# A fused decoder layer: self-attention with centred weights, scores on row halves, another order on VectorE and TensorE

## The chip, the cores and the metric

The kernel is one program on one core of a Trainium2 chip. The metric is the device time of one execution in microseconds (us). Engines are named as in the profile: PE is TensorE's matmuls (PEld its weight loads), DVE is VectorE, ACT is ScalarE, POOL is GpSimd, SP is SyncE.

## The reference, cut to what matters

One decoder layer on x of shape 4 x 512 x 256: causal self-attention with a squared feature map (16 heads of 16 features), cross-attention to 1601 context rows, and a top-2 mixture of 8 experts, with a layer norm after each. Only the first part is touched:

```python
def _feature_map(x, gamma, beta):                 # x: one head's 16 features
    mu = x.mean(axis=-1, keepdims=True)
    var = ((x - mu) ** 2).mean(axis=-1, keepdims=True)
    xn = (x - mu) / jnp.sqrt(var + LN_EPS) * gamma + beta
    ...
q = hidden @ Wq.T ; k = hidden @ Wk.T ; v = hidden @ Wv.T      # 16 heads x 16
phi_q, phi_k = _feature_map(q), _feature_map(k)
# causal: num = phi_q . cumsum(phi_k v), den = phi_q . cumsum(phi_k) + EPS
y = num / den ; return y @ Wo.T
```

The features' inner product is the square of (xn_q . xn_k) / 4, so the kernel squares a score matrix instead of forming 136 features.

## The kernel before, in words

**Stages.** Self-attention of all four batches comes first (0 to about 331 us of the profile), then cross-attention, then the experts. Every engine runs its own hand-written list of instructions in order, and semaphores join them.

**Slots.** A batch of 512 tokens has four row tiles of 128 and four quads of four heads. A batch runs as 16 slots, slot n = 4g + c: quad g, key tile c. In slot n PE makes the scores of slot n+1 (L1417, four heads, 512, 384, 256 or 128 query columns for c = 0 to 3) into PSUM banks 4 and 5 in turn, ACT squares them into A (L751), POOL masks the diagonal block (L550), and PE multiplies the values of slot n into bank 6 (L1427). DVE copies bank 6 out at a quad's end (`quad_out`, L1010).

**Work alongside.** `alongside` (L422) hangs other steps on the slots, and each engine walks the same list. *rest*: the last steps of the batch before (back, yt, out, stats, rsqrt, norm) in slots 0 to 7. *own*: transposes of later quads' q and k (`turn`, L1398; ACT copies qT, DVE copies kT). *ahead*: the features of the next batch. For each row tile i PE projects q and k (`project_qk`, bank 2, six 512-column matmuls) and v (`project_v`, bank 3, six 256-column ones) in slot 2i+1. In slot 2i+2 DVE centres (`centre`: sum, scale, subtract, L954 to L958) and ACT copies v and squares the centred values (L692, L694). In slot 2i+3 DVE forms the variance, in slot 2i+4 ACT takes the root (`deviation`, L698) and DVE normalises (L973 to L980), in slot 2i+5 DVE applies gamma and beta, and slots 9 to 12 split the result into high and low parts. Batches 0 to 2 carry such work for the next one; batch 3 carries weight casts instead.

**Waits that matter.** `project_qk` of tile i waits for `cen_ok` of tile i-1, since bank 2 must be read. A score matmul waits for the square that last read its bank, two matmuls earlier. The opening (L448) runs the same steps for batch 0 before any slot, tile by tile. kT holds four slabs a quad: each head's keys on its own 64 rows with zeros on the other 64 (two memsets, L935 and L936), so a score matmul contracts over 128 rows and DVE copies each transposed pair twice (L1003, L1004).

## Time and profile before

| what | value |
|---|---|
| median of the timed runs | 1490.67 us (1488.88 to 1492.04, 3 runs) |
| the profiled execution | 1501.86 us, its span 1500.1 us, mean granted clock 0.899 |
| PE busy / DVE / ACT / POOL | 83% / 50% / 39% / 46% of the span |
| self-attention, first to last instruction | about 335 us |
| one batch of self-attention, with the next one's features alongside | about 65 to 72 us |

Read the page for the shares first, then the stretches of self-attention alone, then the timeline of one batch. PE's busy time is modelled from pipelined matmuls, so the starts of instructions are the safer numbers. A timeline row is: start, duration, engine, line, operation, tiles, shape, count, and in brackets the idle time before it with what ended it.

### The profile page before, as it was taken

The numbers are of one execution on the slowest core, as the hardware profiler recorded it, in microseconds if no ns is written. First come the engines' busy times: TensorE is split into PE (matmuls) and PEld (weight loads), VectorE is DVE, ScalarE is ACT, GpSimd is POOL, SyncE is SP. The second block draws the span as 40 slices with busy tenths as digits, with TensorE's granted clock in tenths as the row PEclk, the third lists the DMA queues.
The fourth block names the chain that finished last, engine by engine and source line by source line (L and its number), as shares of the span: only waits on it lengthen the run. The fifth ranks groups of instructions, "written<-read, shape, count | busy, mean of one in ns | idle before, by whom it ended". The sixth has DMA issues, their size and how long they took to land.

```text
span 1500.1 us, 20297 instructions
## 1 busy us (share of the span) xinstructions
PE 1243.3 (83%) x6416; PEld 712.3 (47%) x6416; DVE 754.2 (50%) x1328; ACT 582.5 (39%) x999; POOL 684.5 (46%) x597
## 2 busy tenths in 40 slices
PE   3488778856999899998999989999994449999970
PEld 3355454534554445544455444554543426666640
DVE  6475858536335753458624665446423432222217
ACT  3364555632444544445434444444441012222210
POOL 0132323420467674676655766666794431111111
PEclk8688897966999999999999999999996569999995
DMA  5580000010000100000000000000002921111113
GB/s 172 197 270 16 1 0 0 1 45 11 1 0 1 36 10 1 1 1 23 22 2 1 1 11 23 1 0 1 1 1 83 316 68 42 44 46 42 45 43 143
DMA packets 33007, 64.66 MB, mean 43 GB/s; under 512 B 4221, under 2 KB 22398, under 8 KB 32640
## 3 DMA queue, kind: packets, MB, share of 16 engines
q1 hardware_dynamic: 23200, 32.41, 6.6%
q10 hardware_dynamic: 6304, 22.59, 4.7%
q0 software_dynamic: 3408, 8.43, 1.6%
q8 instruction: 55, 0.90, 0.2%
q14 instruction: 40, 0.33, 0.1%
HBM read 52.89 MB, written 28.34 MB: 54 GB/s over the span
## 4 chain that ended last, share of the span: by engine, by line
PE 60%; DVE 20%; issue 10%; ACT 3%; POOL 2%; DMA 2%; another core or an unknown queue 1%; ACTq 1%; SPq 0%; DVEq 0%; POOLq 0%
PE PS L1582 11%; PE PS L1689 9%; PE PS L1510 9%; PE PS L1593 8%; DVE mxp L1168 5%; PE PS L1706 5%; PE PS L225 3%; PE PS L1417 2%; PE PS L1523 2%; PE PS L226 2%; PE PS L227 2%; DVE R L1148 2%; PE PS L1406 2%; PE PS L1427 2%; POOL acc L608 1%
## 5 line engine op out<-in xcount | busy, mean ns | idle before, releaser
L608 POOL TENSOR_TENSOR acc<-acc,PX 128x1024 f32<-128x1024 f32 (+1 forms) x176 | 421.2, 2393 | 161.1 <-ACT PX L846 155.2
L846 ACT ACTIVATE PX<-PS 128x1024 f32<-128x1024 f32 (+1 forms) x208 | 212.9, 1025 | 247.2 <-PE PS L1582 236.4
L1168 DVE TENSOR_REDUCE mxp<-PS 128x2 f32<-128x804 f32 x256 | 240.4, 986 | 132.3 <-PE PS L1523 131.9
L1593 PE MATMUL PS<-PX,V 128*64 128x512 f32 (+1 forms) x832 | 226.3, 623 | 0.0
L550 POOL TENSOR_SCALAR_AFFINE_SELECT A<-A 128x128 f32<-128x128 f32 x256 | 88.8, 359 | 219.8 <-ACT A L751 216.2
L1689 PE MATMUL PS<-W,XBT 128*128 x312 | 149.6, 603 | 1.3 <-ACT XBT L902 1.3
L751 ACT ACTIVATE A<-PS 128x512 f32<-128x512 f32 (+3 forms) x256 | 99.3, 437 | 98.0 <-PE PS L1417 90.9
L669 POOL DMA_INDIRECT Y<-yb,goal_u x39 | 38.4, 986 | 201.8 <-DVE yb L1327 196.7
L1417 PE MATMUL PS<-qT,kT 128*128 128x512 f32 (+3 forms) x256 | 88.0, 420 | 27.0 <-ACT A L751 21.9
L1582 PEld LDWEIGHTS PS<-QH,KH 64*128 64x128 f32 (+1 forms) x416 | 38.4, 181 | 151.3 <-issue 89.9
L1582 PE MATMUL PS<-QH,KH 64*128 64x512 f32 (+1 forms) x416 | 104.6, 499 | 3.5 <-issue 2.2
L1523 PE MATMUL PS<-KH,QH 64*128 64x402 f32 x512 | 79.0, 369 | 18.5 <-DVE mxp L1168 18.5
L1582 PE MATMUL PS<-QH,KL 64*128 64x512 f32 (+1 forms) x416 | 83.3, 395 | 0.0
L1582 PE MATMUL PS<-MR,one_row 64*128 64x512 f32 (+1 forms) x416 | 83.2, 393 | 0.0
L1582 PE MATMUL PS<-QL,KH 64*128 64x512 f32 (+1 forms) x416 | 83.2, 395 | 0.0
L1417 PEld LDWEIGHTS PS<-qT,kT 128*128 128x128 f32 x256 | 48.9, 218 | 64.3 <-ACT A L751 47.6
L605 POOL TENSOR_TENSOR acc<-PX 128x1024 f32<-128x1024 f32 x16 | 38.0, 2376 | 90.5 <-ACT PX L846 90.5
L1689 PEld LDWEIGHTS PS<-W,XBT 128*128 128x128 f32 x312 | 57.2, 194 | 43.3 <-issue 41.4
L1706 PE MATMUL PS<-W,hT 128*128 x312 | 73.9, 380 | 0.8 <-ACT hT L915 0.8
L1321 DVE TENSOR_TENSOR hm<-PS,gl 128x512 f32<-128x512 f32 x39 | 27.0, 691 | 94.2 <-PE PS L1689 94.2
L1193 DVE TENSOR_TENSOR X<-PS,X 128x512 f32<-128x512 f32 (+1 forms) x32 | 22.1, 692 | 102.9 <-PE PS L227 102.8
L829 ACT COPY V<-PS 128x512 f32<-128x512 f32 (+1 forms) x52 | 30.5, 587 | 103.7 <-PE PS L1510 103.7
(261 smaller groups left out, 2138.9 us busy)
## 6 DMA issues: line engine op xcount, KB each, us to landing
W<-in_w SPq DMA_DIRECT2D x24, 512.0 KB
XB<-XG ACTq DMA_DIRECT2D x39, 129.0 KB, 2.1
yl<-Y SPq DMA_DIRECT2D x4, 1024.0 KB, 9.0
X<-in_x SPq DMA_DIRECT2D x1, 2048.0 KB, 12.1
out<-X SPq DMA_DIRECT2D x4, 512.0 KB, 2.9
xt_raw<-in_xt SPq DMA_DIRECT2D x3, 512.0 KB, 4.4
c_raw<-in_ctxt SPq DMA_DIRECT2D x6, 200.0 KB, 2.4
c_raw<-in_ctxt SPq DMA_DIRECT2D x12, 100.0 KB, 2.6
```

The costliest lines, as they stand in the source:

```text
L550: pool.affine_select(out=blk, in_=blk, compare_op=ALU.is_ge, fill=0.0, base=0, pattern=[[1, P]], channel_multiplier=-1).then_inc(mask_ok, 1)
L608: ins = pool.tensor_tensor(sums[0:r], sums[0:r], PX[0:r, (NL * p + t) % NP, :, :], ALU.add)
L751: act.activation(A[:, u % 8, P * c:T], PS[:, 4 + u % 2, P * c:T], ACT.Square, scale=0.25).then_inc(sqr_ok, 1)
L846: act.activation(PX[0:r, u % NP, :, :], PS[0:r, score_buffer(u):score_buffer(u) + 2, :], ACT.Exp, scale=XD ** -0.5)\
L1168: dve.tensor_reduce(mxp[:, p % 2, :, v % NT, v // NT:v // NT + 1].rearrange("p a o -> p (a o)"), PS[:, k:k + 2, 0:BW], AX, ALU.max)\
L1417: pe.matmul(PS[:, 4 + u % 2, P * c:T], kT[:, g % 2, j, P * c:P * c + P], qT[:, g % 2, j // 2, P * c:T], start=True, stop=True).then_inc(sc ...
L1510: mm = pe.matmul(o, l, r, start=(n == 0), stop=(n == len(ops) - 1))
L1523: mm = pe.matmul(bank(bk + half, BW), QH[rows, p % 2, P * i:P * i + P], KH[rows, p % 2, BSTART[k]:BSTART[k] + BW], start=True, stop=True)
L1582: mm = pe.matmul(bank(score_buffer(u) + half, rows=r), lhs, q_[rows, p % 2, :], start=(n == 0), stop=(n == 3))
L1593: mm = pe.matmul(PS[rows, 4, :], V[0:LROWS[j], j, P * p + XD * half:P * p + XD * half + XD], PX[0:LROWS[j], u % NP, half, :], start=(j == ...
L1689: mm = pe.matmul(bank(2 * m + j % 2), XBT[:, j % 2, c, :], W13[:, bass.ds(e, 1), m, c, :].rearrange("p o n -> p (o n)"), start=(c == 0), s ...
L1706: mm = pe.matmul(bank(6, D), hT[:, j % 2, f, :], W2[:, bass.ds(e, 1), f, :].rearrange("p o n -> p (o n)"), start=(f == 0), stop=(f == FC - 1))
```

## The change

1. **Centred weights.** Subtracting a head's mean over its 16 features is linear, so DVE centres the columns of Wq and Wk once, ahead of the casts (two sums, a scale, two additions of 128x512). `centre` goes on DVE. ACT squares bank 2 directly. `normalise` now multiplies the projection in PSUM, so it is the last reader of the bank: `project_qk` of tile i waits for `nrm_ok` of tile i-1.
2. **Row halves.** kT has two slabs without zeros (the memsets go). The two heads of a pair are two matmuls on 64 rows each, into banks 4 and 5; ACT squares both banks in one instruction; a pair of scores waits for the squares of the pair before. DVE copies kT once.
3. **Order.** In `alongside` the variance moves to slot 2i+2, normalise to 2i+3, gamma and beta to 2i+4. On DVE a slot's feature steps come ahead of `quad_out`. On PE projections come last in a slot, behind the value products. The opening goes two tiles at a time, with bank 6 as a second bank.

```diff
-            for i in range(NT):
-                for after, kind in ((1, "project v"), (1, "project qk"), (2, "centre"), (3, "variance"), (4, "normalise"), (5, "affine")):
+            for i in reversed(range(NT)):
+                for after, kind in ((1, "project v"), (1, "project qk"), (2, "variance"), (2, "centre"), (3, "normalise"), (4, "affine")):
...
+        for two in ((0, 1), (2, 3)):
+            OPENING += [(kind, i) for i in two for kind in FEATURES[0:3]] + [("variance", i) for i in two]
+            OPENING += [("split", i - 2) for i in two if i >= 2]
+            OPENING += [("normalise", i) for i in two] + [("affine", i) for i in two]
...
# ACT
-                act.wait_ge(cen_ok, NT * t + i + 1)
-                act.activation(feat[:, i, :], cen[:, i % 2, :], ACT.Square).then_inc(sq_ok, 1)
+                act.wait_ge(qk_mm, NT * t + i + 1)
+                act.activation(feat[:, i, :], bank(qk_bank(t, i)), ACT.Square).then_inc(sq_ok, 1)
...
-                for j in range(4):
-                    u, c = 4 * n + j, n % NT
-                    act.wait_ge(sc_mm, 64 * b + u + 1)
+                for two in range(2):
+                    u, c = 4 * n + 2 * two, n % NT
+                    act.wait_ge(sc_mm, 64 * b + u + 2)
...
-                    act.activation(A[:, u % 8, P * c:T], PS[:, 4 + u % 2, P * c:T], ACT.Square,
-                                   scale=0.25).then_inc(sqr_ok, 1)
+                    act.activation(A[:, u % 8:u % 8 + 2, P * c:T], PS[:, 4:6, P * c:T], ACT.Square,
+                                   scale=0.25).then_inc(sqr_ok, 2)
...
# DVE
-            dve.memset(as32(kT[64:P, :, 0:4:2, :]), 0.0).then_inc(const_dve, 1)
-            dve.memset(as32(kT[0:64, :, 1:4:2, :]), 0.0).then_inc(const_dve, 1)
+            dve.wait_ge(ld_q, 16)
+            for c in range(KC):
+                ins = dve.tensor_reduce(w_mean[:, c, :], groups[c], AX, ALU.add)
+            ins.then_inc(wch, 1)
+            dve.wait_ge(wch, 1)
+            dve.tensor_scalar(w_mean[:, :, :], w_mean[:, :, :], -1.0 / SF, None, ALU.mult).then_inc(wch, 1)
+            dve.wait_ge(wch, 2)
+            for c in range(KC):
+                ins = dve.tensor_tensor(groups[c], groups[c], w_mean[:, c, :].unsqueeze(2).broadcast_to([P, 32, SF]), ALU.add)
...
-                dve.tensor_tensor(v, v, rs.unsqueeze(2).broadcast_to([P, 32, SF]), ALU.mult).then_inc(nrm_ok, 1)
+                if started(t, i, 2):
+                    dve.wait_ge(feat_ok, NT * t + i - 1)
+                dve.tensor_tensor(v, bank(qk_bank(t, i)).rearrange("p (g f) -> p g f", f=SF), rs.unsqueeze(2).broadcast_to([P, 32, SF]), ALU.mult).then_inc(nrm_ok, 1)
...
-                dve.tensor_copy(kT[0:64, g % 2, 2 * q, :], bank(1, rows=64)).then_inc(kT_ok, 1)
-                dve.tensor_copy(kT[64:P, g % 2, 2 * q + 1, :], PS[64:P, 1, :]).then_inc(kT_ok, 1)
+                dve.tensor_copy(kT[:, g % 2, q, :], bank(1)).then_inc(kT_ok, 1)
...
-                    if n % NT == NT - 1:
-                        quad_out(b, n // NT)
                     for d, s in steps:
                         if s[0] not in LATE and s[0] != "x":
                             step(b + d, s)
+                    if n % NT == NT - 1:
+                        quad_out(b, n // NT)
...
# PE
-                if started(t, i, 1):
-                    pe.wait_ge(cen_ok, NT * t + i)
+                if isinstance(t, int) and t == 0:
+                    if i >= 2:
+                        pe.wait_ge(nrm_ok, i - 1)
+                else:
+                    pe.wait_ge(nrm_ok, NT * t + i)
...
                 if started(b, u, 2):
-                    pe.wait_ge(sqr_ok, 64 * b + u - 1)
-                pe.matmul(PS[:, 4 + u % 2, P * c:T], kT[:, g % 2, j, P * c:P * c + P],
-                          qT[:, g % 2, j // 2, P * c:T], start=True, stop=True).then_inc(sc_mm, 1)
+                    pe.wait_ge(sqr_ok, 64 * b + u)
+                for half in range(2):
+                    rows = slice(64 * half, 64 * half + 64)
+                    pe.matmul(PS[:, 4 + half, P * c:T], kT[rows, g % 2, two, P * c:P * c + P],
+                              qT[rows, g % 2, two, P * c:T], start=True, stop=True).then_inc(sc_mm, 1)
...
-                    half = (len(steps) + 1) // 2
+                    steps.sort(key=lambda ds: ds[1][0] in ("project qk", "project v"))
+                    half = min((len(steps) + 1) // 2, sum(s[0] not in ("project qk", "project v") for d, s in steps))
```

PE, batch 0, slots 2 and 3, before: the scores of slot 4 (128x512), the two transposes (q and k of a head pair), slot 3's values (32x128) and the projection of tile 1 of the next batch. xt_h and xt_l are the high and low parts of x, WSh and WSl those of the weights, QX and KX the features, VS the values, A the squared scores.

```order
L1417 MATMUL PS<-qT,kT 128x512 [waits sqr_ok,kT_ok,qT_ok]
L1417 MATMUL PS<-qT,kT 128x512 [waits sqr_ok]
L1406 MATMUL PS<-ident,QX 128x128 [waits qT_ok]
L1406 MATMUL PS<-ident,QX 128x128 x3
L1406 MATMUL PS<-ident,KX 128x128 [waits kT_ok]
L1406 MATMUL PS<-ident,KX 128x128 x3
L1417 MATMUL PS<-qT,kT 128x512 [waits sqr_ok] x2
L1427 MATMUL PS<-A,VS 32x128 [waits mask_ok] x4
L225 MATMUL PS<-WSh,xt_h 128x512 [waits cen_ok,xt_lo]
L226 MATMUL PS<-WSl,xt_h 128x512
```

The same place now:

```order
L1426 MATMUL PS<-qT,kT 128x512 [waits sqr_ok,kT_ok,qT_ok]
L1426 MATMUL PS<-qT,kT 128x512
L1412 MATMUL PS<-ident,QX 128x128 [waits qT_ok]
L1412 MATMUL PS<-ident,QX 128x128 x3
L1412 MATMUL PS<-ident,KX 128x128 [waits kT_ok]
L1412 MATMUL PS<-ident,KX 128x128 x3
L1426 MATMUL PS<-qT,kT 128x512 [waits sqr_ok]
L1426 MATMUL PS<-qT,kT 128x512
L1436 MATMUL PS<-A,VS 32x128 [waits mask_ok] x4
L225 MATMUL PS<-WSh,xt_h 128x512 [waits nrm_ok,xt_lo]
L226 MATMUL PS<-WSl,xt_h 128x512
```

The projection stood behind `cen_ok` of tile 0, from slot 2; it now stands behind `nrm_ok` of tile 0, which DVE gives in slot 3 itself. Both scores of a pair now share one wait.

DVE, batch 0, slots 2 and 3, before: centring of tile 0 (L954 to L958), the quad's values out (L1010), variance, the two kT copies.

```order
L954 TENSOR_REDUCE g_mean<-PS 128x32 [waits qk_mm]
L955 TENSOR_SCALAR g_mean<-g_mean 128x32 [waits cch]
L958 TENSOR_TENSOR cen<-PS,g_mean 128x512 [waits feat_ok,cch]
L1010 COPY osb<-PS 128x512 [waits av_mm]
L963 TENSOR_REDUCE g_var<-feat 128x32 [waits sq_ok]
L965 TENSOR_SCALAR g_var<-g_var 128x32 [waits vch]
L1003 CAST kT<-PS 64x512 [waits tk_mm]
L1004 CAST kT<-PS 64x512
```

The same place now:

```order
L967 TENSOR_REDUCE g_var<-feat 128x32 [waits sq_ok]
L969 TENSOR_SCALAR g_var<-g_var 128x32 [waits vch]
L977 RECIPROCAL g_rs<-g_sd 128x32 [waits sd_ok]
L978 TENSOR_TENSOR g_t<-g_rs 128x32 [waits fch]
L979 TENSOR_TENSOR g_t<-g_t,g_var 128x32 [waits fch]
L980 TENSOR_SCALAR g_t<-g_t 128x32 [waits fch]
L981 TENSOR_TENSOR g_rs<-g_rs,g_t 128x32 [waits fch]
L986 TENSOR_TENSOR cen<-PS,g_rs 128x512 [waits feat_ok,fn_ok]
L1015 COPY osb<-PS 128x512 [waits av_mm]
L1009 CAST kT<-PS 128x512 [waits tk_mm]
```

The whole of normalise (`g_rs` to `cen<-PS,g_rs`) moved one slot forward, ahead of the quad's copy, and centring is gone.

## Rows read from the trace of the kernel before

**Rows 1.** Busy time by stretch: two quads of batch 2, one of batch 3
```profile
core 0: us, PE busy (x) PEld busy (x) DVE busy (x) ACT busy (x) POOL busy (x), PEclk, DMA share, GB/s
197.90:216.60 18.70, 15.36 (x105) 10.60 (x105) 8.24 (x15) 9.73 (x25) 5.40 (x16) 0.91 0.00 0
236.50:255.40 18.90, 15.10 (x76) 8.09 (x75) 17.31 (x41) 12.14 (x31) 6.92 (x19) 0.74 0.00 0
269.50:281.80 12.30, 11.29 (x90) 7.55 (x91) 5.67 (x11) 7.96 (x22) 4.30 (x15) 1.00 0.00 1
```

**Rows 2.** Waits of batch 2: engine line waited for, us, times, longest
```profile
ACT A L751 <- PE PS L1417: 27.3, 23, 5.2
...
ACT feat L694 <- DVE cen L958: 3.6, 2, 2.6
...
PE PS L225 <- DVE xt_l L942: 2.2, 1, 2.2
```

**Rows 3.** Timeline, PE (start, us): first value products of slots 0, 8, 0; 0, 3, 8, 0
```profile
63.49 1.08 PE L1427 MATMUL PS<-A,VS 128*32 128x512 f32 x4
...
99.89 1.06 PE L1427 MATMUL PS<-A,VS 128*32 128x512 f32 x8
...
128.75 0.64 PE L1427 MATMUL PS<-A,VS 128*32 128x512 f32 x4
...
200.05 1.06 PE L1427 MATMUL PS<-A,VS 128*32 128x512 f32 x8
...
216.01 0.42 PE L1427 MATMUL PS<-A,VS 128*32 128x128 f32 x8
...
240.19 1.07 PE L1427 MATMUL PS<-A,VS 128*32 128x512 f32 x8
...
271.62 1.07 PE L1427 MATMUL PS<-A,VS 128*32 128x512 f32 x8
```

**Rows 4.** Timeline, all engines, around the second projection of batch 2
```profile
215.36 0.72 PE L1417 MATMUL PS<-qT,kT 128*128 128x512 f32 x2
...
215.88 1.09 ACT L751 ACTIVATE A<-PS 128x512 f32<-128x512 f32 x2 [2.63 <-PE PS L1417]
...
216.36 0.50 PE L225 MATMUL PS<-WSh,xt_h 128*128 128x512 f32 x1
```

**Rows 5.** The page's costliest groups: ScalarE reading two banks at once
```profile
L846 ACT ACTIVATE PX<-PS 128x1024 f32<-128x1024 f32 (+1 forms) x208 | 212.9, 1025 | 247.2 <-PE PS L1582 236.4
```

**Rows 6.** Timeline, ACT and DVE: deviation to the end of normalise
```profile
244.17 0.21 ACT L698 ACTIVATE g_sd<-g_var 128x32 f32<-128x32 f32 x1
...
244.41 0.35 DVE L973 RECIPROCAL g_rs<-g_sd 128x32 f32<-128x32 f32 x1 [0.81 <-ACT g_sd L698]
...
245.69 0.69 DVE L980 TENSOR_TENSOR cen<-cen,g_rs 128x512 f32<-128x512 f32 x1
```

**Rows 7.** Timeline, PE: two projection matmuls of the third projection of batch 2
```profile
226.98 0.63 PE L226 MATMUL PS<-WSl,xt_h 128*128 128x512 f32 x1
...
227.41 0.63 PE L227 MATMUL PS<-WSh,xt_l 128*128 128x512 f32 x1
```

**Rows 8.** Timeline, PE, cross-attention: matmul pairs on row halves
```profile
509.78 0.50 PE L1582 MATMUL PS<-QH,KH 64*128 64x512 f32 x2
...
510.12 0.40 PE L1582 MATMUL PS<-QL,KH 64*128 64x512 f32 x2
...
510.35 0.40 PE L1582 MATMUL PS<-QH,KL 64*128 64x512 f32 x2
```

**Rows 9.** Timeline, the opening: ACT's first cast, PE's first matmul, first transposes
```profile
6.45 1.47 ACT L680 CAST WSh<-raw 128x1536 fp32r<-128x1536 f32 x1 [3.82 <-DMA raw<-in_wqkv]
...
11.00 0.77 PE L225 MATMUL PS<-WSh,xt_h 128*128 128x512 f32 x1 [11.00 <-DVE xt_l L942]
...
48.09 1.12 PE L1406 MATMUL PS<-ident,QX 128*128 128x128 f32 x4 [15.67 <-DVE KX L998]
```

**Rows 10.** Timeline, PE: a transpose behind the second copy of kT
```profile
241.99 0.55 PE L1406 MATMUL PS<-ident,KX 128*128 128x128 f32 x3 [0.73 <-DVE kT L1004]
```

More of the change, by code:

```diff
@@ L765, in _ @@
                 if s == ("x",):
+                    act.wait_ge(wch, 3)
+                    act.copy(WSh[:, :, 0:3 * D], raw[:, 0:2, 0:3 * D]).then_inc(w_hi, 1)
                     act.wait_ge(ld_w, 16 * N_LDW)
@@ L1408, in turn, with scores @@
                 mm.then_inc(done, 1)
-            def score(b, n, j):
-                g, c, u = n // NT, n % NT, 4 * n + j
-                if c == 0 and j == 0:
+            def scores(b, n, two):
+                g, c, u = n // NT, n % NT, 4 * n + 2 * two
+                if c == 0 and two == 0:
                     pe.wait_ge(qT_ok, 8 * b + 2 * g + 2)
-                    pe.wait_ge(kT_ok, 16 * b + 4 * g + 4)
+                    pe.wait_ge(kT_ok, 8 * b + 2 * g + 2)
                 if started(b, u, 2):
-                    pe.wait_ge(sqr_ok, 64 * b + u - 1)
-                pe.matmul(PS[:, 4 + u % 2, P * c:T], kT[:, g % 2, j, P * c:P * c + P],
-                          qT[:, g % 2, j // 2, P * c:T], start=True, stop=True).then_inc(sc_mm, 1)
+                    pe.wait_ge(sqr_ok, 64 * b + u)
[3 more added lines that the diff above has]
+                              qT[rows, g % 2, two, P * c:T], start=True, stop=True).then_inc(sc_mm, 1)
             def value(b, n, j):
@@ L1476, in attention @@
                     steps = [(d, s) for d, s in alongside(n, first, more) if s[0] in PE_STEPS]
-                    half = (len(steps) + 1) // 2
-                    for j in range(4):
+                    steps.sort(key=lambda ds: ds[1][0] in ("project qk", "project v"))
+                    half = min((len(steps) + 1) // 2, sum(s[0] not in ("project qk", "project v") for d, s in steps))
+                    for two in range(2):
                         if n + 1 < SLOTS:
-                            score(b, n + 1, j)
+                            scores(b, n + 1, two)
                         elif more:
-                            score(b + 1, 0, j)
-                        if j == 1:
+                            scores(b + 1, 0, two)
+                        if two == 0:
                             for d, s in steps[:half]:
@@ L1492, in _ @@
                 step(0, s)
-            for j in range(4):
-                score(0, 0, j)
+            for two in range(2):
+                scores(0, 0, two)
             attention(0, True, True)
```

49 lines of the change are left out of this document (19 added, 30 removed).

## The prediction

> **What bounds the kernel now.** The change touches self-attention alone, so the page's shares of the whole span say little. I read the busy times of single quads first [rows 1], then the waits of batch 2 [rows 2], then the timeline of that batch [rows 3, 4]. In [rows 1] no engine is full: PE is the busiest (15.4 of 18.7 us), but its busy time is modelled and overlaps. The one other full engine is DVE in a quad with feature work, 17.3 of 18.9 us. [rows 2] says ACT waits 27.3 us of a batch for score matmuls. So a batch is a chain of hand-overs: PE scores, ACT squares, PE again, and PE's in-order steps stand between. What counts is what a step puts on PE's queue between two score pairs. [rows 3] gives the lengths of it: batch 2 takes 200.05 to 271.62, 71.6 us, of which slots 0 to 3 take 16.0, slots 3 to 8 24.2 and slots 8 to the next 0 31.4. Batch 0 takes 65.3 (63.49 to 128.75). The profiled execution is 11.2 us above the median; I sum changes against it and move them to the median unscaled.
>
> **The new wait, worked out.** PE's projection of tile i (slots 3, 5, 7) now waits for normalise of tile i-1 in the same slot. DVE needs ACT's root for that, and the root stands on ACT behind the squares of this slot's last score pair. So from that pair's start the chain is: 0.52 us until ACT starts (215.36 to 215.88) [rows 4], 1.03 for a square over two banks of 512 [rows 5], 2.21 from the root to the end of normalise (244.17 to 245.69 + 0.69) [rows 6]: 3.76 us. Before, the projection started 1.00 us after that pair (216.36) [rows 4]. That is +2.76 in slots 3 and 7. In slot 5 the pair is 256 wide: about 0.41 + 0.55 + 2.21 = 3.17, less some 1.0 of value products and pair that PE has anyway, +2.2. Together **+7.7 us a batch**. Queued behind the wait are the v projection and then the next slot's scores, so ACT, POOL and DVE run dry as well: nothing covers it. Ends: +4 if a third of each chain falls where PE waited anyway, +9 if in slot 5 DVE is still at the layer statistics.
>
> **The clock of those projections.** A 512-column matmul steps by 0.43 us at the lower level (1.2 GHz) [rows 7], which here stands behind a PE wait, and by 0.23 at the higher (2.4 GHz) [rows 8]. A tile's q, k and v are six of 512 and six of 256 columns: 2.1 us or 3.8. After a wait of 2 to 3 us I expect the lower level for part of each: take +1.0 for each of three, **+3.0**, ends 0 and +5.1.
>
> **What is taken away.** (a) In slot 1 PE sat 2.2 us before the first projection for xt_l [rows 2], ahead of the second score pair; now pair and values come first and fill it: **-1.5**, ends 0 and -2.2. (b) ACT's square waited 3.6 us a batch for centring [rows 2], once 2.6 us in slot 8 with the score squares behind it; now it reads PSUM: **-2.5**, ends 0 and -3.6. Centring itself (some 1.6 us a tile on DVE) is otherwise hidden, and so costs nothing to remove. (c) The second kT copy is 0.7 us. Where a transpose waits for it (0.73) [rows 10], at slots 8 and 15 and the quad's turn, it goes: **-2.1**, ends 0 and -5.5 (all eight).
>
> **Score pairs.** In cross-attention two matmuls on row halves step together by 0.23 us for 512 columns (510.12 to 510.35) [rows 8], so a pair takes what one took. Where PE sets the pace (quads 0 and 1, 10240 columns) half goes: 2.3 at full clock, take **-2.0**. Against it: before, PE refilled one bank while ACT squared the other, and ACT could run two squares in 1.09 us without a gap [rows 4]. Now both banks are freed at once, and a pair costs 1.03 + 0.52 + 0.15 (hand-over, my estimate) = 1.70: +0.61 at 512 wide, less when other ACT work fills the gap. Take +0.4 for 8 of a batch's 32 pairs, **+3.2**, ends 0 and +6. DVE's order (feature steps before the quad's copy) adds a delay of osb, which the value products of the next quad reach later than the projection; hidden, up to 0.7 a quad if not.
>
> **Sum of a batch with features alongside:** 7.7 + 3.0 - 1.5 - 2.5 - 2.1 - 2.0 + 3.2 = **+5.8**. Laying the slots of batch 2 out by hand with these durations gives 14.4, 33.0 and 29.5 us against 16.0, 24.2 and 31.4: +5.3, where the last stretch is 27.2 at the higher clock throughout and about 31 at the lower. Three such batches: +17.4.
>
> **Batch 3** has no projections. 20 exposed pairs x 0.4 = 8.0, half the columns of four quads -4.6, one kT copy a quad -2.9: **+0.5**, ends -5 and +6. In [rows 1] its quad has the full clock and PE 11.3 of 12.3 us busy, so PE-paced pairs are many there.
>
> **The opening.** Centring the weights is two sums, a scale and two additions, about 3.0 us on DVE by the 0.69 us of a 128x512 operation [rows 6], ahead of ACT's first cast at 6.45 [rows 9]; it hides nothing, so PE starts at 13.9 instead of 11.0. The memsets that go ended before the weights landed: nothing. DVE then leaves out four centrings (6.2 us), but going by pairs of tiles it waits about 2.6 us for the second square of each pair. The transposes, at 48.09 [rows 9] behind DVE's last split, come about 0.6 earlier, and one kT copy helps once: **-1.0**, ends -4 and +3.
>
> **Total:** 17.4 + 0.5 - 1.0 = +16.9, that is 1518.8 for an execution like the profiled one and **1507.6 for the median**.
>
> **A rule beside the rows.** The first pair on row halves after matmuls of another tile shape took 0.34 us to the next, the following 0.23 [rows 8]: 0.11 for the change of shape. Score pairs now differ in shape from the transposes and output matmuls between them, some 24 more changes a batch. The Trainium skill, "TensorEngine Tiling (Array Packing)", section "Key Properties", says that changing the tiling mode, not merely the tile, drains the engine; that speaks against this change, and by it the row's 0.11 would be paid at each. I left it out of the sum since most such changes fall where PE waits for ACT; it is a rival below.
>
> **Rivals.**
> - *The gains meet a high clock (no change).* No lower level at the projections (0 for 3.0) and half the exposed pairs: 1.2 a batch, 3.6 - 1.0 - 3.5 (batch 3) = -0.9: 1489.8. For it: quad 0 of batch 2 had 0.91 of the full clock [rows 1]. Against: the new waits are longer than the ones before. 0.12.
> - *DVE's queue is the pace (faster).* In quads 1 and 2 DVE is 17.3 of 18.9 us busy [rows 1]. If its backlog sets their length, three centrings (4.7) and four copies (2.8) come off, and two of the three new waits lie within DVE's own queue and cost nothing: -7.5 + 2.8 = -4.7 a batch, -14.1 - 1.0 = -15: 1475.6. It decides if DVE's idle there, 1.6 us, is all the slack there is. Against: only 3.6 us of ACT's waiting names centring [rows 2]; the rest names PE. 0.16.
> - *The lower clock stays.* PE works less, waits longer and is at 1.2 GHz through most of a batch: projections +5.1, exposed pairs +6.0, some +0.4 more: 11 a batch, +33, batch 3 +4.5, opening -1: 1527. [rows 1] has 0.74 in one quad already. 0.08.
> - *Every change of shape is paid* at 0.11: 2.6 a batch, 9.7 in all: 1517. 0.04.
>
> **How the numbers follow.** The forecast has 0.60 (slower), and its own range by the ends above is about 1497 to 1518. Faster has 0.16 from DVE's queue and 0.02 from the forecast's low ends; within 0.2% (3 us, about what a measurement of this kernel can tell from no change) 0.12 and 0.01; slower 0.69. The range goes from 1480, which leaves out most of the DVE case, to 1522, which leaves out the lasting low clock: together about 0.17.
>
> **What would show it.** In the trace after: PE idle of 2 to 3 us before the first q/k projection matmul in slots 3, 5 and 7, named as a wait for normalise; slots 3 to 8 of batch 2 at 31 to 34 us, slots 0 to 3 at 14.5; no ACT wait for DVE in slot 8; PE's first matmul near 13.9 and the first transposes near 47.5. It is wrong if those waits are under 1 us, which would mean that ACT reaches the root sooner than the last pair allows, or if slots 8 to 0 fall below 26 us.

## The result, and the profile after

The changed kernel takes 1522.02 us, median of four runs (1520.49 to 1523.09), against 1489.78 us for the kernel before (1486.94 to 1492.04, four runs). The ratio is 1.0217, 95% interval 1.0196 to 1.0237: 32 us slower. The profiled execution took 1520.49 us. The forecast had the direction, but +17 us (1507.6) instead of +32; 1522.02 lies just outside its range of 1480 to 1522.

Read self-attention by batch first. These are the busy times of the kernel after, each stretch (from:to, its length, then the engines' busy us and counts) from a batch's first value products to the next one's. The last one ends at the last copy of a quad (L1015).

```profile
core 0: us, PE busy (x) PEld busy (x) DVE busy (x) ACT busy (x) POOL busy (x), PEclk, DMA share, GB/s
60.35:131.19 70.84, 52.37 (x322) 29.88 (x321) 33.06 (x73) 35.60 (x65) 19.98 (x65) 0.84 0.57 189
131.19:210.28 79.09, 58.85 (x355) 35.64 (x353) 38.60 (x91) 36.69 (x67) 20.72 (x66) 0.81 0.03 8
210.28:288.38 78.10, 57.30 (x354) 34.88 (x352) 38.51 (x91) 36.49 (x67) 20.89 (x66) 0.83 0.00 0
288.38:338.79 50.41, 39.89 (x266) 19.00 (x264) 18.61 (x39) 26.69 (x41) 18.44 (x61) 0.80 0.12 34
```

The same view of a second execution of the kernel before (1495.36 us, profiled beside the experiments):

```profile
62.09:125.74 63.65, 51.61 (x322) 31.46 (x321) 44.02 (x91) 37.86 (x98) 21.14 (x64) 0.88 0.65 218
125.74:197.80 72.06, 57.48 (x353) 35.97 (x353) 50.96 (x113) 39.45 (x100) 24.65 (x65) 0.86 0.03 9
197.80:268.85 71.05, 57.31 (x353) 35.84 (x353) 50.23 (x109) 39.17 (x100) 23.95 (x65) 0.86 0.00 0
268.85:311.16 42.31, 36.93 (x265) 21.11 (x264) 22.73 (x46) 28.42 (x70) 20.43 (x59) 1.00 0.09 26
```

I use this second execution as the base from here on. The one that the prediction had read took 1501.86 us and 65.3, 71.3, 71.6 and 44.7 us for the four batches ([rows 3]; the last one ends with the copy at 316.4). The second took 63.7, 72.1, 71.1 and 42.3. After is 70.8, 79.1, 78.1 and 50.4: +7.2, +7.0, +7.1 and +8.1, or 29.4, less 1.7 in the opening (the first column starts at 60.35 instead of 62.09). DVE's busy time fell by 11 to 12 us in each of the first three batches and PE has nearly the same number of matmuls as before (the counts in brackets), yet every batch is longer. The first three have a granted clock (PEclk) of 0.84, 0.81 and 0.83 instead of 0.88, 0.86 and 0.86. Batch 3 has 0.80 instead of 1.00.

Where in a batch? Starts of value products of the kernel after, batch 2, slots 0, 3, 8 and the next 0, which answer to [rows 3]:

```profile
210.28 1.25 PE L1436 MATMUL PS<-A,VS 128*32 128x512 f32 x8
...
224.06 0.43 PE L1436 MATMUL PS<-A,VS 128*32 128x128 f32 x8
...
260.90 1.07 PE L1436 MATMUL PS<-A,VS 128*32 128x512 f32 x8
...
288.38 1.06 PE L1436 MATMUL PS<-A,VS 128*32 128x512 f32 x8
```

Slots 0 to 3 take 13.8, slots 3 to 8 36.8, the rest 27.5. In the second execution of before they took 15.9, 24.3 and 30.8 (batches 0 and 1 go the same way: slots 3 to 8 take 32.3 and 35.3 instead of 21.5 and 24.2). The first and last stretch gained 2.2 and 3.3; the middle, where the projections of tiles 1 to 3 stand, lost 12.5. Here is its first projection, slot 3 of the kernel after; it answers to [rows 4, 6]:

```profile
223.63 0.49 PE L1426 MATMUL PS<-qT,kT 64*128 64x512 f32 x2
...
224.25 1.02 ACT L755 ACTIVATE A<-PS 128x1024 f32<-128x1024 f32 x1 [3.29 <-issue]
...
225.17 0.22 ACT L702 ACTIVATE g_sd<-g_var 128x32 f32<-128x32 f32 x1
...
225.42 0.35 DVE L977 RECIPROCAL g_rs<-g_sd 128x32 f32<-128x32 f32 x1 [4.33 <-ACT g_sd L702]
...
226.79 0.69 DVE L986 TENSOR_TENSOR cen<-PS,g_rs 128x512 f32<-128x512 f32 x1
...
227.53 0.80 PE L225 MATMUL PS<-WSh,xt_h 128*128 128x512 f32 x1 [3.05 <-DVE cen L986]
...
228.13 0.63 PE L226 MATMUL PS<-WSl,xt_h 128*128 128x512 f32 x1
...
231.67 0.69 PE L1426 MATMUL PS<-qT,kT 64*128 64x384 f32 x2
...
232.56 0.81 ACT L755 ACTIVATE A<-PS 128x768 f32<-128x768 f32 x1 [6.70 <-PE PS L1426]
```

The score pair starts at 223.63 and ACT squares both banks (224.25). Only then comes the root (225.17), DVE works from 225.42 to the end of `cen`, and PE, done with the value products at about 224.5, starts the projection at 227.53 after 3.05 us of nothing. The matmuls that follow take 0.63 us each and step by 0.43 (228.13, then 228.56), the 1.2 GHz level. The projection is through after 4.14 us. The next score pair stands behind all twelve, at 231.67, and ACT waited 6.70 us for it. From score pair to score pair that is 8.04 us. In the kernel before the same stretch took 3.21:

```profile
213.10 0.72 PE L1417 MATMUL PS<-qT,kT 128*128 128x512 f32 x2
...
216.31 0.52 PE L1417 MATMUL PS<-qT,kT 128*128 128x384 f32 x2
```

The waits between 60 and 310 us say that this is not one place. Kernel after:

```profile
ACT A L755 <- PE PS L1426: 99.9, 66, 7.3
...
PE PS L225 <- DVE cen L986: 25.7, 9, 3.1
```

Kernel before:

```profile
ACT A L751 <- PE PS L1417: 84.6, 83, 5.2
...
ACT feat L694 <- DVE cen L958: 11.5, 6, 2.6
...
PE PS L225 <- DVE xt_l L942: 6.9, 3, 2.6
```

Nine waits for `cen` (three a batch) hold 25.7 us of PE. ACT's 11.5 us for centring and PE's 6.9 us for `xt_l` are gone. ACT's wait for scores grew by 15.3. The twelve matmuls of the nine projections in slots 3, 5 and 7 took 35.0 us together, from the first of them to what PE starts next, against 22.4 for the same matmuls in the second execution of before.

### The profile page after: what moved, and what is told of

The parts are those of the page before. It is cut to its first block, busy times and chain, and to the rows that moved or that the text cites. A ratio compares the mean times of both kernels' runs of the same rounds, so it can differ in the third digit from the quotient of the medians.

```text
span 1518.7 us, 19910 instructions
## 1 busy us (share of the span) xinstructions
PE 1242.6 (82%) x6416; PEld 701.8 (46%) x6416; DVE 708.2 (47%) x1251; ACT 572.1 (38%) x871; POOL 672.8 (44%) x597
## 4 chain that ended last, share of the span: by engine, by line
PE 51%; DVE 12%; issue 7%; POOL 4%; DMA 2%; ACT 2%; SPq 0%; DVEq 0%; ACTq 0%; POOLq 0%
PE PS L1592 11%; PE PS L1699 9%; PE PS L1520 9%; PE PS L1603 8%; DVE mxp L1171 5%; PE PS L1716 4%; PE PS L1533 2%; POOL XG L669 2%; DVE R L1151 2%; PE PS L225 2%; POOL acc L614 1%; PE PS L1708 1%; DVE Cc L1121 1%; PE PS L1573 1%; DMA c_raw<-in_ctxt 1%
## 5 line engine op out<-in xcount | busy, mean ns | idle before, releaser
L556 POOL TENSOR_SCALAR_AFFINE_SELECT A<-A 128x128 f32<-128x128 f32 x256 | 78.6, 328 | 254.2 <-ACT A L755 253.8
L755 ACT ACTIVATE A<-PS 128x1024 f32<-128x1024 f32 (+3 forms) x128 | 90.4, 706 | 149.2 <-PE PS L1426 113.6
L1426 PE MATMUL PS<-qT,kT 64*128 64x512 f32 (+3 forms) x256 | 59.9, 464 | 39.7 <-ACT A L755 35.8
L1533 PEld LDWEIGHTS PS<-KH,QH 64*128 64x128 f32 x512 | 50.1, 191 | 42.9 <-DVE mxp L1171 31.9
```

The costliest lines, as they stand in the source:

```text
L556: pool.affine_select(out=blk, in_=blk, compare_op=ALU.is_ge, fill=0.0, base=0, pattern=[[1, P]], channel_multiplier=-1).then_inc(mask_ok, 1)
L755: act.activation(A[:, u % 8:u % 8 + 2, P * c:T], PS[:, 4:6, P * c:T], ACT.Square, scale=0.25).then_inc(sqr_ok, 2)
L1426: pe.matmul(PS[:, 4 + half, P * c:T], kT[rows, g % 2, two, P * c:P * c + P], qT[rows, g % 2, two, P * c:T], start=True, stop=True).then_in ...
L1533: mm = pe.matmul(bank(bk + half, BW), QH[rows, p % 2, P * i:P * i + P], KH[rows, p % 2, BSTART[k]:BSTART[k] + BW], start=True, stop=True)
```

## The experiments

Four questions: is it the wait, how much of it is the clock, what is the rest of the change worth, and can the gain be had. Each timed kernel is compared with runs of the kernel before on its own chip, whose medians were 1498.04, 1495.66 or 1497.82 us (1489.78 for the result above). So ratios are given, and a difference in us is that of two ratios times 1496. They are the recorded estimates with their 95% intervals; two medians divided can come out up to 0.002 away (0.9868 and not 0.9884 for the last row of the table), so nothing is read from differences that small. The table also has the end of self-attention and the length of its batches in each trace. What follows the last copy of a quad is the same in all and took 1177 to 1188 us, so a few us between two ratios prove little unless the traced batches agree.

| kernel | ratio | self-attention ends | batches 0 to 2 | batch 3 |
|---|---|---|---|---|
| before (second execution) | 1 | 311.2 | 206.8 | 42.3 |
| after | 1.0217, 1.0202 | 338.8 | 228.0 | 50.4 |
| after, bank copied early | 0.9998 | 311.8 | 199.3 | 51.2 |
| after, PE kept busy | 1.0137 | 322.2 | 211.6 | 49.4 |
| after, root first | 1.0112 | 329.5 | 216.6 | 51.4 |
| after, a square a bank | 1.0111 | 333.4 | 229.1 | 44.2 |
| after, old DVE order | 1.0174 | 343.5 | 233.8 | 49.6 |
| root first, a square a bank, old DVE order | 1.0141 | 330.1 | 225.4 | 44.7 |
| before, row halves alone | 1.0024 | 312.8 | 202.3 | 47.4 |
| before, centred weights alone | 0.9961 | 307.7 | 201.5 | 43.6 |
| early copy, a square a bank | 0.9932 | 301.7 | 197.1 | 44.4 |
| the same, old DVE order | 0.9884 | 294.3 | 190.9 | 43.6 |

**The control.** The kernel after, unchanged, beside the second group.

> The changed kernel once more, unedited, on the chip of the runs beside it, as their yardstick. The runs of a1 to a4 shared a chip on which the kernel before took 1498 us, not 1490. If the change costs the same there: ratio 1.02 to the kernel before, and its self-attention ends at 339 us of the profile as in the first one, give or take 4.

Ratio 1.0202 (1.0176 to 1.0227), +30 us; its trace has self-attention ending within 0.2 us of the first one (338.62), while all behind that took 1186.5 us instead of 1179.9. The kernel before, once more, for its trace:

> The kernel before once more, unedited, for a second profile. In the first one its self-attention ended (last copy of a quad) at 316.4 us, with 71.3 and 71.6 us for batches 1 and 2. If the granted clock falls by chance, these move by a few us (311 to 321), and the low clock sits at other slots.

1495.36 us. Its self-attention is 5.2 us shorter than in the first execution, and 2.4 of them lie in the last quad of batch 3. Busy times of that quad in the second execution:

```profile
303.09:311.16 8.07, 6.90 (x48) 3.32 (x48) 2.77 (x5) 5.01 (x14) 4.34 (x14) 1.00 0.48 133
```

And in the first:

```profile
305.87:316.35 10.48, 9.30 (x48) 4.38 (x48) 2.77 (x6) 5.00 (x14) 4.39 (x14) 0.67 0.53 152
```

It took 8.1 us at a granted clock of 1.00, against 10.5 at 0.67.

**The wait alone removed.** DVE copies the bank before normalise, so the bank is free early; centred weights, row halves and both orders stay.

> The changed kernel with one thing put back: DVE copies the projection of a tile out of PSUM in slot 2i+2 (one 128x512 copy, some 0.7 us), and the next projection waits for that copy and for the square, not for normalise in its own slot. Theory A (PE's wait for normalise in slots 3, 5 and 7, and the low clock of the projections behind it, is the loss): slots 3 to 8 of batch 2 fall from 36.8 us to about 22 to 25, three batches give back 33 to 40 us, so 1483 to 1490. Rival B (what costs is that both score banks are freed together): the wait goes but the time stays above 1515. Rival C (the loss is spread over the new order of steps): half of it comes back, about 1505.

```diff
+            def centre(t, i):                                  # DVE, slot 2i+2, ahead of variance
+                dve.wait_ge(sq_ok, NT * t + i + 1)
...
+                dve.tensor_copy(cen[:, i % 2, :], bank(qk_bank(t, i))).then_inc(cen_ok, 1)
...
-                dve.tensor_tensor(v, bank(qk_bank(t, i)).rearrange("p (g f) -> p g f", f=SF), rs...
+                dve.tensor_tensor(v, v, rs...
...
-                    pe.wait_ge(nrm_ok, NT * t + i)             # PE, project_qk
+                    pe.wait_ge(cen_ok, NT * t + i)
+                    pe.wait_ge(sq_ok, NT * t + i)
```

Ratio 0.9998 (0.9982 to 1.0014): the whole loss is gone, with one more 0.69 us copy a tile on DVE. The same slot in its trace (score pair, projection, next score pair):

```profile
206.40 0.79 PE L1435 MATMUL PS<-qT,kT 64*128 64x512 f32 x2
...
207.48 0.50 PE L225 MATMUL PS<-WSh,xt_h 128*128 128x512 f32 x1
...
209.78 0.44 PE L1435 MATMUL PS<-qT,kT 64*128 64x384 f32 x2
```

3.38 us from pair to pair. No PE wait for DVE's `cen` is left, and the projection is through in 2.30 us (207.48 to 209.78) instead of 4.14. (One of its nine projections, in slot 5 of batch 1, still ran at the lower level and took 3.99 us.) So the wait with what follows it costs 30 to 33 us by the ratios (1.0202 or 1.0217 less 0.9998) and 28.7 by the traces of batches 0 to 2 (228.0 less 199.3), 3.2 to 3.6 for each of nine. Not all of what the rows show is net: slots 3 to 8 of the three batches lost 35.2 us of their length with the copy (104.5 to 69.3), while their other slots grew by 6.4 (123.5 to 130.0). The cost of the added copies is in these numbers too and was not measured by itself.

**The wait kept, PE kept busy.** Fourteen matmuls of 256 columns, whose result nobody reads, fill the wait.

> The changed kernel, with 14 matmuls of 256 columns into an unused half of bank 3 put before PE's wait for normalise in slots 3, 5 and 7 (their result is not read). They fill 1.6 us of the wait at 2.4 GHz, 3.0 at 1.2 GHz. If the clock of the projections is a price of its own (a projection took 4.1 us there against 2.1), nine projections come back by up to 2 us: about 1504 to 1510. If the granted clock does not rise, or the wait alone is the loss: 1520 or, with the filler late, up to 1530.

```diff
+                    for _ in range(14 if i >= 1 else 0):
+                        pe.matmul(PS[:, 3, D:2 * D], xt_h[:, 0, 0:P], WSh[:, 0, 0:D], start=True, stop=True)
                     pe.wait_ge(nrm_ok, NT * t + i)
```

Ratio 1.0137 (1.0120 to 1.0154). The same slot in its timeline: score pair, filler, first projection matmul, next score pair.

```profile
214.66 0.50 PE L1428 MATMUL PS<-qT,kT 64*128 64x512 f32 x2
...
215.45 1.93 PE L1388 MATMUL PS<-WSh,xt_h 128*128 128x256 f32 x14
...
218.57 0.50 PE L225 MATMUL PS<-WSh,xt_h 128*128 128x512 f32 x1 [1.20 <-DVE cen L986]
...
220.89 0.44 PE L1428 MATMUL PS<-qT,kT 64*128 64x384 f32 x2
```

The projection starts 3.91 us after the pair, as without filler (3.90), so DVE's `cen` comes no sooner. But it is through after 2.32 us (218.57 to 220.89) instead of 4.14, and pair to pair is 6.23 us instead of 8.04. Busy times from slot 3 to slot 8 of batch 2, this kernel:

```profile
215.09:245.48 30.39, 24.42 (x177) 17.53 (x175) 19.06 (x51) 10.70 (x20) 6.24 (x21) 1.00 0.00 0
```

The kernel after:

```profile
224.06:260.90 36.84, 25.80 (x135) 17.69 (x133) 19.05 (x51) 10.69 (x20) 6.35 (x21) 0.72 0.00 0
```

Clock 1.00 against 0.72, and 30.4 us against 36.8, with work added. All nine projections are at the higher level now (20.6 us together instead of 35.0). The low clock therefore costs 10 to 12 us by the ratios and 16.4 by the traces of batches 0 to 2: a third of what the wait costs by the one, over half by the other. The rest is idle time.

**Root first.** If ACT takes the root ahead of the slot's squares, normalise need not wait for them.

> The changed kernel with one ACT step moved: the root (`deviation`) of slot 2i+3 ahead of that slot's squares, not behind them. Nothing is copied, and PE still waits for normalise of its own slot. If that wait is the loss because the root stands behind the last pair's squares (theory A): the 3 us waits in slots 3, 5 and 7 shrink to 1 or less, slots 3 to 8 of batch 2 fall from 36.8 to 26 to 30 us, and 20 to 28 of the 30 us come back: 1497 to 1505 where the kernel before takes 1496. If the chain on DVE is itself too long to hide (variance must come first, 0.9 us): 8 to 15 back, above 1508.

```diff
+                    for d, s in alongside(n, first, more):
+                        if s[0] == "normalise":
+                            step(b + d, s)                     # ACT: deviation
                     squared_scores(b, n + 1)
                     for d, s in others_first(alongside(n, first, more)):
-                        step(b + d, s)
+                        if s[0] != "normalise":
+                            step(b + d, s)
```

Ratio 1.0112 (1.0087 to 1.0137): about half of the loss back, less than I expected. Its waits from 60 to 310 us:

```profile
PE PS L225 <- DVE cen L990: 8.4, 7, 2.7
...
ACT g_sd L702 <- DVE g_var L973: 7.8, 12, 1.0
```

Its timeline, DVE and PE, at slot 5 of batch 2:

```profile
227.81 1.40 DVE L1043 BATCH_NORM_STATS2 ln_st<-X 128x6 f32 x4
...
229.80 0.35 DVE L981 RECIPROCAL g_rs<-g_sd 128x32 f32<-128x32 f32 x1
...
231.82 0.80 PE L225 MATMUL PS<-WSh,xt_h 128*128 128x512 f32 x1 [2.05 <-DVE cen L990]
```

In slot 5 normalise (229.80) stands on DVE behind the layer statistics of the batch before (227.81 to 229.9), which the root's time does not change, and ACT now waits 7.8 us for the variance.

**Root first, with the old DVE order and a square a bank.** I took this for the cheap repair: the root early as in the last experiment, and two more edits.

> c1 with a square for each head and VectorE's old order: b4 with the early root in place of the copy. It saves DVE 16 copies of 0.7 us but keeps PE's wait for normalise in its own slot. If what is left of that wait is under 1 us: level with b4, 1472 to 1478. If 1 to 2 us of it stay at each of nine places, and the lower clock with them: 1482 to 1492.

```diff
+                    for d, s in alongside(n, first, more):
+                        if s[0] == "normalise":
+                            step(b + d, s)                     # ACT: deviation
...
+                    if n % NT == NT - 1:
+                        quad_out(b, n // NT)                   # DVE, ahead of the slot's other steps
                     for d, s in steps:
```

The square a bank is that of the experiment further down.

Ratio 1.0141 (1.0111 to 1.0171), worse than the last, a plain miss. Its waits from 60 to 310 us:

```profile
PE PS L225 <- DVE cen L990: 25.2, 9, 4.0
```

Its timeline at slot 3 of batch 2:

```profile
217.37 0.23 ACT L702 ACTIVATE g_sd<-g_var 128x32 f32<-128x32 f32 x1 [0.49 <-DVE g_var L973]
...
221.51 0.69 DVE L1019 COPY osb<-PS 128x512 f32<-128x512 f32 x1 [3.57 <-PE PS L1440]
...
224.22 0.79 PE L225 MATMUL PS<-WSh,xt_h 128*128 128x512 f32 x1 [2.87 <-DVE cen L990]
```

The root is there at 217.6, four microseconds early. But `quad_out` (221.51) stands ahead of normalise again and waited 3.57 us for the value products of this very slot, so PE waits 2.87 us for normalise as before. In this slot the change's DVE order is the partner of its wait: it is needed where PE waits for normalise. This kernel also differs from the last one by its squares, so how much of the 1.0141 against 1.0112 is the order isn't separated.

**DVE's order put back alone.**

> The changed kernel with VectorE's old order: the quad's values are copied out first, then the slot's feature work. Batch 3 grew by 6 us, and in it DVE stands behind a weight cast of ACT before it copies the quad out (2.2 us at 313.4), with the next quad's value products waiting for that copy. If the order is the cause there: batch 3 falls by 2 to 4 us. In batches 0 to 2 the copy then stands ahead of normalise, which PE waits for: 0.7 us more in slots 3 and 7, +4 in all, or nothing, since the root comes later than the copy. Together -4 to +3 against the changed kernel.

```diff
+                    if n % NT == NT - 1:
+                        quad_out(b, n // NT)
                     for d, s in steps:
                         if s[0] not in LATE and s[0] != "x":
                             step(b + d, s)
-                    if n % NT == NT - 1:
-                        quad_out(b, n // NT)
```

Ratio 1.0174 (1.0130 to 1.0218), with self-attention 4.7 us longer in the trace: not to be told from the change in either direction. While the root stands behind the squares, neither order brings normalise sooner by much: in slot 3 of batches 1 and 2 PE waits 3.05 and 3.06 us for it (2.87 and 3.05 with the change's order), and only in slot 7 of these batches 3.98 instead of 2.96.

**Parts of the change on the kernel before.** Row halves alone (both matmuls of a pair on 64 rows, one square for two banks, one kT copy, no memsets):

> The kernel before with the row halves alone: two 64-row matmuls a pair, one square over two banks, one kT copy, no memsets; centring, slots and orders are those of before. Theory A: the parts nearly cancel (half the score columns and a kT copy against a later handover of the banks), -6 to +8 us, so 1484 to 1498. Rival B: +15 to +25 us, 1505 to 1515.

```diff
-                for j in range(4):
-                    act.wait_ge(sc_mm, 64 * b + u + 1)
-                    act.activation(A[:, u % 8, P * c:T], PS[:, 4 + u % 2, P * c:T], ...
+                for two in range(2):
+                    act.wait_ge(sc_mm, 64 * b + u + 2)
+                    act.activation(A[:, u % 8:u % 8 + 2, P * c:T], PS[:, 4:6, P * c:T], ...
...
-                dve.tensor_copy(kT[0:64, g % 2, 2 * q, :], bank(1, rows=64)).then_inc(kT_ok, 1)
-                dve.tensor_copy(kT[64:P, g % 2, 2 * q + 1, :], PS[64:P, 1, :]).then_inc(kT_ok, 1)
+                dve.tensor_copy(kT[:, g % 2, q, :], bank(1)).then_inc(kT_ok, 1)
```

Ratio 1.0024 (1.0000 to 1.0048). In its trace batches 0 to 2 take 62.5, 71.2 and 68.6 us, 4.5 less than before, and batch 3 takes 47.4, 5.1 more. Centred weights alone, where `centre` is one copy and every order is the old one:

> The kernel before with centred weights alone: DVE centres Wq and Wk once, and `centre` is one copy out of PSUM in place of sum, scale and subtraction, 0.9 us less a tile; slots, orders, score matmuls and squares are those of before. Theory: DVE's work there was mostly hidden, ACT waited 3.6 us a batch for it, and the opening pays about 3 us for the weights and gets 3.6 back: -2 to -8 us, 1488 to 1494. If DVE's queue had been the pace of quads 1 and 2: -12 us or more.

```diff
-                chain(dve.tensor_reduce(g_mean[:, i % 2, :], v, AX, ALU.add), cch, at + 1)
-                chain(dve.tensor_scalar(g_mean[:, i % 2, :], g_mean[:, i % 2, :], -1.0 / SF, None, ALU.mult), cch, at + 2)
-                dve.tensor_tensor(cen[:, i % 2, :]..., v, g_mean[:, i % 2, :]..., ALU.add).then_inc(cen_ok, 1)
...
+                dve.tensor_copy(cen[:, i % 2, :], bank(2)).then_inc(cen_ok, 1)
```

The edit of the weights ahead of the casts is the one of the change. Ratio 0.9961 (0.9940 to 0.9981), -6 us, and batches 0 to 2 are 1.8 us shorter each on average in the trace.

**A square for each bank.** The kernel after, with the two score matmuls on row halves, but each bank squared and freed on its own.

> The changed kernel with a square for each head again, so that each score bank is freed on its own, while the matmuls stay on row halves. Theory A: 0 to -10 us (most of it in batch 3, which grew by 5.7 us), 1512 to 1522. Rival B: the loss comes back, -20 us or more, 1500 or below.

```diff
-                for two in range(2):
-                    act.wait_ge(sc_mm, 64 * b + u + 2)
-                    act.activation(A[:, u % 8:u % 8 + 2, P * c:T], PS[:, 4:6, P * c:T], ...
+                for j in range(4):
+                    act.wait_ge(sc_mm, 64 * b + u + 1)
+                    act.activation(A[:, u % 8, P * c:T], PS[:, 4 + u % 2, P * c:T], ...
...
-                if started(b, u, 2):
-                    pe.wait_ge(sqr_ok, 64 * b + u)
                 for half in range(2):
+                    if started(b, u, 2):
+                        pe.wait_ge(sqr_ok, 64 * b + u + half - 1)
```

Ratio 1.0111 (1.0088 to 1.0134). Its batches 0 to 2 together are no shorter, but batch 3 is. ACT's wait for scores in batch 3 is 15.4 us (20 waits) instead of 20.7 (19). The last two quads of batch 3 in this kernel:

```profile
314.20:325.62 11.42, 9.35 (x59) 4.58 (x58) 5.10 (x9) 8.47 (x21) 5.90 (x17) 0.88 0.01 2
325.62:333.38 7.76, 6.93 (x45) 2.80 (x44) 1.54 (x6) 3.07 (x10) 3.29 (x12) 0.74 0.69 197
```

Batch 3 takes 44.2 us instead of 50.4. Of these 6.2 us, 5.1 lie in these two quads (19.2 instead of 24.3), whose clock rose too, from 0.64 and 0.50 to 0.88 and 0.74. So the 6.2 are what the later hand-over costs with the clock that falls behind it; no run parts the two. The ratio improved by 14 to 16 us, self-attention in the trace by 5.4 (5.2 against the control's). The whole span is 5.1 us shorter than in the first trace of the kernel after and 11.5 shorter than in the control's, and the difference between these two lies behind self-attention, where nothing was edited. I rely on the 6.2 of batch 3 and leave the other part open.

**What can be had.** The first experiment's early copy with a square a bank, in the change's DVE order:

> The combination of b4 without VectorE's old order (DVE copies the projection out, one square a head, new order). b3 said that the order alone is worth nothing with the wait in place. If that holds without the wait too: within 3 us of b4, 1473 to 1480. If the order matters once nothing hides it (batch 3 with its weight casts above all): 1480 to 1488.

Its edits are those of the early copy and of the square a bank together. Ratio 0.9932 (0.9911 to 0.9952). The same in the old DVE order (`quad_out` first):

> The projection copied out by DVE as in a1, a square for each head as in a4, VectorE's old order as in b3: all that seemed to cost is put back, and the centred weights, row halves, one kT copy and the new slots stay. Theory A: a1 tied with the kernel before, a4 gave back 6 to 9 us of 32, so this is 5 to 12 us faster than the kernel before (ratio 0.992 to 0.997). If the parts do not add up, because the batch is paced by something else once the wait is gone: within 0.2% of it.

Ratio 0.9884 (0.9854 to 0.9914), 1475.94 us beside 1495.66: faster than both kernels, and by more than the 5 to 12 us that I had expected. With the wait gone the old DVE order is the better one, by some 7 us in the ratios, whose intervals just meet and which come from two chips, and by 7.4 in the ends of self-attention in the traces.

## Why the prediction was right in direction and short in size

**The wait: right in place, near in price.** Predicted 2.76, 2.2 and 2.76 us in slots 3, 5 and 7, 7.7 a batch, 23.1 for three. Batch 2 has 3.05, and in slots 5 and 7 of the kernel after:

```profile
243.04 0.80 PE L225 MATMUL PS<-WSh,xt_h 128*128 128x512 f32 x1 [2.68 <-DVE cen L986]
...
254.56 0.79 PE L225 MATMUL PS<-WSh,xt_h 128*128 128x512 f32 x1 [2.96 <-DVE cen L986]
```

That is 8.7, and 25.7 over nine. Slot 5 was the worst guess: the cover of 1.0 that I allowed it was 0.5 less.

**The clock of the projections: right in kind, short in size.** I took +1.0 each, and +9 in all, between 0 and +15.3. All three of batch 2 run at the lower level nearly throughout: in slot 3 4.14 us from the first matmul to the next score pair (227.53 to 231.67) against 2.30 (207.48 to 209.78) where there is no wait. In batches 0 and 1 the first or the last matmuls of some are at the higher level, and those take 3.3 to 3.8. All nine together grew by 12.6 us (22.4 to 35.0), and the filler gave back 10 to 16, where the term had 9.

Wait and clock together, forecast at 3 x 10.7 = 32.1, measured 29 to 33. That this half of the sum holds is in part luck: by the rows it was 25.7 + 12.6 = 38.3, six more than forecast, and "nothing covers it" was not quite so, since other slots grew by 6.4 when the wait went.

**What failed are the credits, that of batch 3 first.** The rest of the change was forecast at 16.9 - 32.1 = -15.2 us. With the wait removed (and a copy a tile added) it measured 0 (0.9998; self-attention ends 0.6 us later than before).
- *Batch 3, forecast +0.5, measured +8.1 (+5.7 against the 44.7 of the execution that the sum was made on).* This is the largest miss of a stage by either. I had 8.0 for the later hand-over of the banks, less 4.6 for half the score columns, less 2.9 for the kT copy. With a square a bank, 6.2 of the 8.0 come back (50.4 to 44.2; 51.2 to 44.4 between the two kernels without the wait), so the cost is real, though part of it comes by the clock. The two credits, 7.5 us together, did not come: even then batch 3 is 44.2, 1.9 above the second execution and 0.5 under the first, and with the row halves alone it takes 47.4. A likely reason is that the PE columns saved stood where PE or ACT waits for the other anyway (in batch 3 ACT waits 20.7 us for scores instead of 12.8, and PE 6.7 for ACT's squares instead of 2.5); no run tests it. That PE is the pace there I had taken from its busy time in one quad [rows 1], and that is a modelled number: in the first quad, at 1.00 in both, it is 11.26 us after and 11.23 before, with half of the score columns gone. In addition the last two quads of the kernel after have a low clock, which the first two do not. Busy times of the last three quads:

```profile
299.18:314.50 15.32, 11.89 (x90) 6.60 (x89) 9.69 (x23) 10.25 (x15) 6.32 (x19) 1.00 0.00 1
314.50:329.25 14.75, 10.58 (x59) 4.12 (x58) 5.11 (x10) 7.83 (x12) 5.34 (x17) 0.64 0.01 1
329.25:338.79 9.54, 8.47 (x46) 3.23 (x44) 1.53 (x5) 2.77 (x5) 3.25 (x12) 0.50 0.63 173
```

  In the second execution of before these three took 12.5, 11.6 and 8.1 us, all at 1.00. The second quad loses 2.8 us at full clock, the third and fourth 4.6 at 0.64 and 0.50. How the 8.1 divides between hand-over and clock beyond that isn't settled.
- *DVE's order, forecast at nothing.* I called the later `osb` hidden, "up to 0.7 a quad if not". Where the wait is gone it costs about 7 us; for the twelve quads with features alongside that is 0.6 each, the bound that I named and did not take. This was measured with a square a bank; that it is the same beside one square for two banks is assumed.
- *Batches 0 to 2, forecast -4.9 a batch beside wait and clock.* The kernel without the wait has 57.5, 72.3 and 69.5, 2.5 a batch less than before. The credit for centring held roughly: -2.5 a batch forecast, and centred weights alone gave 6 us, 1.8 a batch in the traces. The waits for `xt_l` (6.9) and for centring (11.5) vanished from the trace, but while slots 0 to 3 of batches 0 and 2 got 2.2 us shorter each, those of batch 1 got longer (16.4 against 14.7).
- *Opening: -1.0 forecast, -1.7 measured.* PE's first matmul was forecast at 13.9 and stands at 14.36, 0.5 later: ACT's cast waits for the centred weights (L950) and starts at 9.74, where it was 6.45 [rows 9]. The transposes were forecast at 47.5 and start at 44.29, 3.8 us earlier than in [rows 9] and 3.2 earlier than I said. Part of the 3.8 is the execution: in the second one of before they start at 46.87. With centred weights alone they start at 46.57, with the row halves alone at 46.94, so the 2.3 or so that are left come with the opening by pairs of tiles. The next rows are those of the kernel after.

```profile
9.74 1.47 ACT L771 CAST WSh<-raw 128x1536 fp32r<-128x1536 f32 x1 [1.16 <-DVE raw L950]
...
14.36 0.76 PE L225 MATMUL PS<-WSh,xt_h 128*128 128x512 f32 x1 [14.36 <-DVE xt_l L958]
...
44.29 1.12 PE L1412 MATMUL PS<-ident,QX 128*128 128x128 f32 x4 [13.12 <-DVE KX L1004]
```

**The base.** The sum was made against an execution with a granted clock of 0.67 in its last quad of batch 3, 11.2 us over the median, and moved to the median unscaled. Against it self-attention grew by 22.4 us: 19.9 in batches 0 to 2 (forecast 17.4), 5.7 in batch 3 (0.5) and -3.1 in the opening (-1.0). So the batches with features were near on their own base, and batch 3 was not. The second execution ends self-attention 5.2 us sooner, and against it the growth is 27.6: some of what the change loses had been lost in the first one already, 2.4 of it in the quad at 0.67. The whole executions differ by +18.6 and +25.1 us, where the medians differ by +32. The second and the control, profiled beside each other, differ by 31.6: 27.5 in self-attention and 4.1 behind it. So the medians' 32 is self-attention's 27.5 and some 4 us more that fall where nothing was edited; why they do stays open.

**The range.** Its forecast part, 1497 to 1518, is narrower than the ends that it names: the upper ends of a batch's costs alone, 9 + 5.1 + 6, stand 6.2 us above the 7.7 + 3.0 + 3.2 of the sum, or 19 over three batches. The measured time lies within the ends and outside the range.

**The rivals.** DVE's queue as the pace (1475.6, at 0.16) fell: taking out centring's sum and scale gave 6 us, where DVE as the pace would have given 12 or more, and the new waits are PE's, not hidden in DVE's queue. No change (0.12) fell with its assumption: the clock at the projections is the lower level. "The lower clock stays" (1527, at 0.08) is nearest: batches 0 to 2 at 0.81 to 0.84, and the projections at its price. But its +11 a batch and +4.5 in batch 3 were measured as +7.1 and +8.1, so it has the size by other terms. "Every change of shape is paid" (1517): counted in the trace, PE changes shape some 34 times more in batch 2 (24 were forecast), 14 of them in slots 8 to 0, and that stretch fell from 30.8 to 27.5 us; the kernel that beats both has the same tile shapes. The 0.11 us of [rows 8] is not a price of shape alone either: in the kernel with the filler, whose matmuls have the projection's shape, the first projection matmul steps by 0.35 us where PE waited 1.20 (218.57 to 218.92) and by 0.23 in the one place of nine without a wait (160.05 to 160.28). The drain that the Trainium skill states ("TensorEngine Tiling (Array Packing)", "Key Properties") is not refuted, but no run here shows it in the time.

**The signs.** Waits of 2 to 3 us in slots 3, 5 and 7: yes. No ACT wait for DVE in slot 8: yes, it is gone from the list. Slots 3 to 8 of batch 2 at 31 to 34: no, 36.8. Slots 0 to 3 at 14.5: 13.8 in batch 2. Slots 8 to 0 not below 26: 27.5.

## What to carry to other kernels

A step that frees a PSUM bank sets when PE may start again, so its price is not its own duration. It is the whole chain up to it, here square, root, reciprocal, four small operations and normalise, plus a low clock for what PE does next. Taking 1.6 us of mostly hidden work from DVE made PE wait 3. When the last reader of a bank has to move behind a chain, a plain copy ahead of it (0.69 us) keeps the idea without the wait: 0.9998 instead of 1.0217 here, and 0.9884 with a square a bank and the old DVE order beside it.

Credits need the same proof as costs. For each instruction taken away, name the row in which someone waited for it, in that stage; no gain from half of PE's score columns shows in batch 3, where PE and ACT wait for each other.

Reading two banks with one instruction saves ACT little (1.02 us against 1.09 for two) and frees the first bank some half a microsecond late (an estimate, half of the 1.02). Where PE refills banks in turn this cost about 6 us in one batch, the clock that fell with it included.

## What the hardware showed beyond this

Work without a result can pay. Fourteen extra matmuls in each of nine waits (1.92 to 1.94 us in eight of them, 2.87 in one) made the kernel 10 to 12 us faster by the ratios, because the granted clock stayed at 1.00 instead of 0.72 over slots 3 to 8. The prediction had counted the low level for part of a projection (+1.0 us): behind a 3 us wait it lasted for all twelve matmuls in slots 3 and 7 of batch 2 and for eleven in slot 5, while some projections of batches 0 and 1 had a few at the higher level.

Two profiled executions of the same kernel differed by 5.2 us in self-attention: 2.4 of them in the last quad of batch 3, which took 10.5 us at a clock of 0.67 in one and 8.1 at 1.00 in the other. A difference of a few us in one stage should be read from two executions before it is priced.
